# Key transfers shared between two queues, query copies moved to VectorE, and a weight split moved by one pass

## What is computed

```python
qr, qi, kr, ki, v = (heads(x @ W.T) for W in (Wqr, Wqi, Wkr, Wki, Wv))
sr = (einsum('bhqd,bhkd->bhqk', qr, kr) + einsum('bhqd,bhkd->bhqk', qi, ki)) * scale
si = (einsum('bhqd,bhkd->bhqk', qi, kr) - einsum('bhqd,bhkd->bhqk', qr, ki)) * scale
probs = softmax(sqrt(sr * sr + si * si)); ctx = einsum('bhqk,bhkd->bhqd', probs, v)
...
h = h + magnitude_attention(layernorm(h))
h = h + ffn(layernorm(h))      # causal attention, then top-2 routing to 8 experts
```

## Time and profile before

| | |
|---|---|
| time, median of 3 runs | 1024.96 us (1017.67 to 1029.4) |
| profiled execution | 1020.74 us, of which the span is 1018.8 us |
| mean granted TensorE clock | 0.919 of full speed |
| TensorE busy | 897.8 us (88%) |
| VectorE, ScalarE busy | 648.8 us, 651.1 us (64% each) |
| GpSimd busy | 482.7 us (47%) |
| magnitude passes 0 to 7 | about 60 us to 372 us of the span |

### The profile page before, as it was taken

The page is one execution under the profiler, slowest core; times in us unless marked ns, Lnnn a source line. Parts: engine busy times, 40 slices in busy tenths (PEclk is TensorE's granted clock), DMA queues, the critical chain, the costliest instruction groups (busy, mean ns, idle before and its releaser), DMA issues.

```text
span 1018.8 us, 21578 instructions
## 1 busy us (share of the span) xinstructions
PE 897.8 (88%) x7037; PEld 699.2 (69%) x7038; DVE 648.8 (64%) x3050; ACT 651.1 (64%) x1386; POOL 482.7 (47%) x509
## 2 busy tenths in 40 slices
PE   3377979989889879999999999467999999999996
PEld 2254556556556456677777776256999999999896
DVE  1666889889788677678877766673344344343341
ACT  2047879788789788988988888264345345344441
POOL 7677656643001101143334333405677677677654
PEclk7567999899899789999999999757999999999999
DMA  7234233231010200010111102426455456565442
GB/s 205 58 72 82 44 67 65 42 64 31 18 32 14 52 1 2 2 38 2 38 39 38 38 2 69 74 55 107 62 110 99 78 109 88 89 108 91 54 51 32
DMA packets 63299, 59.11 MB, mean 58 GB/s; under 512 B 17471, under 2 KB 54242, under 8 KB 63202
## 3 DMA queue, kind: packets, MB, share of 16 engines
q0 software_dynamic: 25344, 27.89, 19.5%
q1 hardware_dynamic: 37666, 29.76, 11.3%
q10 hardware_dynamic: 192, 0.26, 0.1%
HBM read 35.18 MB, written 16.39 MB: 51 GB/s over the span
## 4 chain that ended last, share of the span: by engine, by line
PE 62%; DVE 13%; SPq 6%; ACT 6%; POOL 5%; issue 4%; DMA 2%; POOLq 0%; DVEq 0%; ACTq 0%
PE ps_scores L776 14%; PE ps_ring L768 11%; PE ps_ring L1044 10%; PE ps_ring L776 6%; SPq L500 5%; PE ps_scores L886 5%; PE ps_ctx L903 5%; PE ps_scores L1044 4%; PE ps_scores L889 4%; POOL got L590 3%; DVE probs L1420 2%; ACT probs L1146 1%; DVE probs L1414 1%; ACT square L1137 1%; DMA k<-k_signed 1%
## 5 line engine op out<-in xcount | busy, mean ns | idle before, releaser
L1260 ACT ACTIVATE probs<-ps_scores,fc_bias 128x512 f32<-128x512 f32 (+1 forms) x144 | 88.9, 617 | 171.5 <-PE ps_scores L776 167.6
L650 POOL DMA_INDIRECT out<-z_t,slots_now x80 | 128.1, 1601 | 83.2 <-DVE z_t L1761 58.9
L768 PE MATMUL ps_ring<-ident,probs 128*128 128x128 f32 x768 | 127.2, 291 | 17.2 <-ACT q L1101 8.0
L1128 ACT ACTIVATE prob_t<-ps_ring 128x512 f32<-128x512 f32 x192 | 114.5, 598 | 37.0 <-PE ps_ring L768 36.3
L1137 ACT ACTIVATE square<-ps_scores 128x512 f32<-128x512 f32 x192 | 104.6, 600 | 29.4 <-PE ps_scores L886 24.2
L1153 ACT ACTIVATE probs<-probs,neg_max 128x128 f32<-128x128 f32 x384 | 120.8, 397 | 2.6 <-DVE neg_max L1420 2.6
L768 PEld LDWEIGHTS ps_ring<-ident,probs 128*128 128x128 f32 x768 | 90.5, 147 | 43.4 <-issue 13.0
L1420 DVE CUSTOM_DVE_ANT_0 probs<-ps_scores,causal 128x128 f32<-128x128 f32 x384 | 88.6, 286 | 40.8 <-PE ps_scores L889 40.5
L1044 PE MATMUL ps_ring<-work,probs 128*128 128x192 f32 x672 | 114.5, 326 | 0.0
L1044 PEld LDWEIGHTS ps_ring<-work,probs 128*128 128x128 f32 x672 | 109.3, 190 | 0.1
L1414 DVE CUSTOM_DVE_ANT_0 probs<-square 128x128 f32<-128x128 f32 x384 | 89.2, 287 | 30.6 <-ACT square L1137 30.1
(11 more groups left out here) (230 smaller groups left out, 2056.1 us busy)
## 6 DMA issues: line engine op xcount, KB each, us to landing
k<-k_signed SPq DMA_DIRECT2D x176, 32.0 KB
work<-pj_w SPq DMA_DIRECT2D x8, 576.0 KB, 4.9
token_in<-xin SPq DMA_DIRECT2D x8, 384.0 KB, 3.4
out<-resid SPq DMA_DIRECT2D x8, 384.0 KB, 4.3
vals<-fc_w SPq DMA_DIRECT2D x8, 384.0 KB, 3.5
vals<-fc_w SPq DMA_DIRECT2D x16, 192.0 KB, 4.1
out<-z_t,slots_now POOLq DMA_INDIRECT x80, 3.6
token_in<-xin SPq DMA_DIRECT2D x8, 128.0 KB, 4.3
```

What stands on the lines that cost most here:

```text
L650: gp.indirect_dma_start(out[:, :], bass.IndirectOffsetOnAxis(slots_now[:, u, 1, t:t + 1], 0), slot_y[:, o, :], None, compute_op=ALU.add).t ...
L768: return pe.transpose(dst, src, ident[0:n, 0:n])
L1128: sc.activation(prob_t[:, s % 2, :, :], src.rearrange("p (h q) -> p h q", h=4), ACT.Exp if p is mag else ACT.Copy).then_inc(ring_free[i], 1)
L1260: sc.activation(hidden[:, c % 2, f_, 0:128 * nt], ps_scores[:, i, 0:128 * nt], ACT.Gelu, bias=fc_bias[:, e, f_:f_ + 1]).then_inc(gelu_done ...
```

## The change

Four things are changed.

Of the 24 key transfers of a group, SyncE keeps all eight of block 0 and the first four of blocks 1 and 2. The other four of blocks 1 and 2 are issued by GpSimd (`turn_rest_of_keys`), at the end of its pass, from group 2 on. Those of group 0 and group 1 stay as they were.

The copy of the last queries (`proj` 5) goes from ScalarE to VectorE, and the shifts of the twelve jobs are laid out anew (`SHIFTS`).

The rounding of the causal weights is cut in three pieces and goes to slots 1, 2 and 3 of pass 7 on ScalarE, the remainders to slots 2, 3 and 4 on VectorE, and TensorE waits piece by piece.

For the first causal group the third and fourth projection go from slots 10 and 13 to 9 and 11.

```diff
+SHIFTS = {13: (0,), 14: (1, 2), 15: (3, 4, 5), 0: (6, 7), 1: (8,), 2: (9,), 3: (10,), 4: (11,)}
 CAU_PROJ = (4, 7, 10, 13)
+FIRST_CAU_PROJ = (4, 7, 9, 11)
...
+        def wait_for_turned_keys(eng, b, g):
+            eng.wait_ge(keys_turned[b], 16 * (8 * g if b == 0 else 4 + 4 * g))
+            if b > 0 and g > 1:
+                eng.wait_ge(late_turned[b - 1], 16 * 4 * (g - 1))
...
@@ SyncE
-                    for quarter, part in product(range(4), range(2)):
+                    for quarter, part in product(range(4 if b == 0 or g == 1 else 2), range(2)):
...
@@ GpSimd, one_pass
                     if fetched is not None and fetched < GROUPS:
                         gather_step(fetched, slot)
+                if 2 <= p + 1 < GROUPS:
+                    turn_rest_of_keys(p + 1)
+
+            def turn_rest_of_keys(g):
+                for b in range(1, BLOCKS):
+                    pool.wait_ge(keys_signed, BLOCKS * g + b + 1)
+                    for quarter, part in product(range(2, 4), range(2)):
+                        to, of = 32 * quarter + HEAD_DIM * part, 32 * quarter + HEAD_DIM * (1 - part)
+                        gp.dma_start(k_of[g % 2][to:to + HEAD_DIM, b, 1, :, :].rearrange("p s k -> p (s k)"),
+                                     k_signed[of:of + HEAD_DIM, b, :]).then_inc(late_turned[b - 1], 16)
...
@@ TensorE
-                        if p is cau and g == 0:
-                            pe.wait_ge(cau_w_split, 2)
                     if p is cau:
                         m, b = divmod(s, 2)
+                        if g == 0:
+                            pe.wait_ge(cau_w_split, m + 1)
...
@@ ScalarE
-                        kind == "proj" and p is mag and s < 3):
+                        kind == "proj" and p is mag and s in (0, 1, 2, 5)):
                     return
...
+            def causal_weights_high(part):
+                raw_qk, raw_v = raw_weights(cau)
+                if part == 0:
+                    act.wait_ge(cau_w_scaled, 4)
+                    for f in (("proj", 5), ("value", 1)):
+                        i, n = PLACE[GROUPS - 1, f]
+                        act.wait_ge(ring_full[i], n + 1)
+                if part < 2:
+                    sc.activation(w_hi[:, :, part, 0:256], raw_qk[:, :, part, :], ACT.Copy).then_inc(cau_w_high, 1)
+                else:
+                    sc.activation(v_hi[:, :, 0:HID], raw_v, ACT.Copy).then_inc(cau_w_high, 1)
...
+                    if p == GROUPS - 1 and 1 <= slot <= 3:
+                        causal_weights_high(slot - 1)
...
-                    split_weights_high(cau_w_scaled, 4, cau_w_high, cau)
...
@@ VectorE
+                elif kind == "proj" and p is mag and s == 5:
+                    dve.wait_ge(ring_full[i], n + 1)
+                    ve.tensor_copy(q_of[number % 2][:, 2, :, :], src.rearrange("p (s k) -> p s k", s=GROUP)
+                                   ).then_inc(free, 1)
...
-                        for j in range(2 * (slot - 13), 2 * (slot - 13) + 2):
+                        for j in SHIFTS[slot]:
                             shift_rows(now, j)
...
+                    if p == GROUPS - 1 and 2 <= slot <= 4:
+                        causal_weights_low(slot - 2)
...
-                    split_weights_low(cau_w_loaded, cau_w_high, cau_w_split, cau)
```

More of the change, by code:

```diff
@@ L104, in causal_fills @@
         fills += [(what, s)] if s is not None else []
-    fills += [("proj", k) for k in range(4) if at == CAU_PROJ[k] - STEPS]
+    fills += [("proj", k) for k in range(4) if at == (FIRST_CAU_PROJ if number == GROUPS else CAU_PROJ)[k] - STEPS]
     fills += [("value", k) for k in range(4) if at == CAU_VALUE[k] - STEPS]
@@ L343, in tower_kernel @@
         keys_turned = [sem(f"keys_turned{b}") for b in range(BLOCKS)]
+        late_turned = [sem(f"late_turned{b}") for b in range(1, BLOCKS)]
         sign_made = sem("sign_made")
@@ L821, in fill @@
                         taken_out(number, ("xT", 0), ("xT", 1))
+                        if p is cau and g == 0:
+                            pe.wait_ge(cau_w_split, 3)
                     for t in range(p.values_per_fill):
@@ L873, in scores @@
                     if g > 0:
-                        pe.wait_ge(keys_turned[j], 8 * 16 * g)
+                        wait_for_turned_keys(pe, j, g)
                     else:
@@ L1200, in one_pass @@
                             turn_rest_of_keys()
+                    if p == GROUPS - 1 and 1 <= slot <= 3:
+                        causal_weights_high(slot - 1)
                     if ready is not None and slot >= 3 and slot % 3 == 0 and slot // 3 <= GROUP:
                         copy_ctx(*phase_of(ready), slot // 3 - 1)
-                if p == GROUPS - 2:
-                    for f in (("proj", 5), ("value", 1)):
-                        i, n = PLACE[GROUPS - 1, f]
-                        act.wait_ge(ring_full[i], n + 1)
-                    split_weights_high(cau_w_scaled, 4, cau_w_high, cau)
             def copy_domains():
@@ L1345, in fill @@
                     elif g > 1:
-                        dve.wait_ge(keys_turned[s], 8 * 16 * (g - 1))
+                        wait_for_turned_keys(dve, s, g - 1)
                     ve.tensor_scalar(k_signed[:, s, :], k[:, s, 0, :, :].rearrange("p s k -> p (s k)"), sign[:, 0:1],
@@ L1605, in split_weights, with causal_weights_low @@
                                  ).then_inc(raw_split, 1)
+            def causal_weights_low(part):
+                raw_qk, raw_v = raw_weights(cau)
+                dve.wait_ge(cau_w_high, part + 1)
+                if part < 2:
+                    ve.tensor_tensor(w_lo[:, :, part, 0:256], raw_qk[:, :, part, :], f(w_hi[:, :, part, 0:256]),
+                                     ALU.subtract).then_inc(cau_w_split, 1)
+                else:
+                    ve.tensor_tensor(v_lo[:, :, 0:HID], raw_v, f(v_hi[:, :, 0:HID]), ALU.subtract
+                                     ).then_inc(cau_w_split, 1)
             def split_first_weights(quarter):
@@ L1629, in one_pass @@
                     if now is not None and now < GROUPS and slot >= 13:
-                        for j in range(2 * (slot - 13), 2 * (slot - 13) + 2):
+                        for j in SHIFTS[slot]:
                             shift_rows(now, j)
-                    if ready is not None and ready < GROUPS and slot < 6:
-                        shift_rows(ready, slot + 6)
+                    if ready is not None and ready < GROUPS and slot < 5:
+                        for j in SHIFTS[slot]:
+                            shift_rows(ready, j)
                     for n, at in ((ready, slot), (before, slot + STEPS)):
```

## The result

The changed kernel takes 1018.59 us in the median (1011.04 to 1025.78, 20 runs); the kernel before took 1024.72 beside it (20 runs). The ratio is 0.9949, 95% interval 0.9928 to 0.9970: 5.2 us faster, where 1025 and no change were forecast. A second comparison, further down, gave 0.9935 (0.9909 to 0.9960).

A forecast was written before the change was run, and what follows sets the result against it. It took TensorE's waits for SyncE's key transfers, ScalarE's query copy and the clock as what could be gained at the borders. Losses of 13.7 us less gains of 12.9 gave +0.8: 1025 us, no measurable change, range 1012 to 1041.

The forecast's parts named there:

- I take somewhat less, 1.10: GpSimd's queue: each plain key transfer costs 1.10 us, so 8.8 us for eight, somewhat under the 1.36 us `word_table` gathers.
- 8.5: Border 1 to 2: GpSimd's late transfers land block 2 at 155.4 where TensorE got it at 146.81, a loss of 8.5 us.
- +0.5, +2.5 and +0.7: Passes 2, 3 and 4: GpSimd's later work, chiefly gathers, moves back behind the transfers, losing 0.5, 2.5 and 0.7 us.
- cheap transfers: Rival: GpSimd transfers at 0.63 us each, clock stays up; 7.1 us gained, 1018 us, or 1012 to 1015; chance 0.2.
- the clock: TensorE's granted clock: stays up at border 4 to 5 (-2.0 us) and 6 to 7 (-2.5), falls at 1 to 2 (+1.5).
- Key waits -3.6: Borders 3 to 4, 4 to 5, 5 to 6: TensorE's three waits for SyncE's key transfers go, 3.6 us gained.
- Query copy -2.0: Borders 0 to 1, 3 to 4, 4 to 5, 5 to 6: ScalarE's copy leaves the row, 0.5 us gained at each.
- I count nothing: Border 2 to 3: group 4's norm, two slots late, waits behind the shifts, so no gain is booked for the query copy.
- Border 6 to 7, -4.7: Weights and query copy off ScalarE's row: -3.2 us, clock -2.5, pieces in slots 1 to 4 +1.0; together 4.7 gained.
- 7 to 8, -0.6: Border 7 to 8: ScalarE's 0.70 us copy of the last causal projection moves to slot 11, where it has room; 0.6 us gained.
- Moments 2.8 us later: Border 1 to 2: group 3's moments begin at 140.5 instead of 137.70, behind VectorE's query copy and three shifts.
- A landing of 2.5: GpSimd's key transfers: the data land 2.5 us after the transfers, a figure used for the block arrivals at border 1 to 2.

The follow-up runs named there:

- second comparison: The changed kernel as it is, timed again against the kernel before on the same chip, beside the later follow-up kernels: ratio 0.9935 (0.9909 to 0.9960).
- half transfers: Changed kernel with each GpSimd key transfer cut in two of half the columns, 16 instead of 8 a group: ratio to the kernel before 1.0032 (1.0008 to 1.0055).
- K alone: Kernel before with only GpSimd's share of the key transfers for blocks 1 and 2, from group 2 on: ratio to it 0.9987 (0.9967 to 1.0007).
- Q: The last query copy on VectorE with the new shifts; as the only change to the kernel before, ratio to it 0.9992 (0.9969 to 1.0015).
- C: Causal weights in three pieces, projections in slots 4, 7, 9, 11; as the only change to the kernel before, ratio to it 0.9970 (0.9949 to 0.9991).
- The kernel without Q: Changed kernel with the last query copy on ScalarE again and the shifts in their old slots: ratio to the kernel before 0.9934 (0.9909 to 0.9959).
- K in the whole: Told by the changed kernel with all 24 key transfers on SyncE again: ratio to the kernel before 1.0017 (0.9992 to 1.0042), 7.0 us slower than the whole change.

## Why the prediction was wrong

**The step that failed** is "I take somewhat less, 1.10" for a transfer of GpSimd. It is 0.49 to 0.51. The bounds were 0.63 below and 1.91 above; the value taken was that of the nearest row of the same engine, a gather over 128 rows, and the true one lay below even the lower bound. Put into the prediction's own sums: block 1 lands at 144.1 + 2.0 + 2.0 = 148.1 instead of 151.0, 4.9 us after it is wanted. That is now the later of the two, since block 2 lands at 150.2 and is wanted, 4.9 us later than before, at 150.6. With the old wait of 1.13 gone, border 1 to 2 costs 3.8 instead of 8.5. The place gathers of pass 3 end in time: in the trace they end at 200.69, the root follows at once and is there at 202.1, and VectorE uses it at 202.56 without a wait:

```profile
199.15 1.54 POOL L599 DMA_INDIRECT got<-place_rows,id_now  x1 [0.30 <-issue]
200.76 0.24 POOL L593 TENSOR_SCALAR rstd<-moments 128x4 f32<-128x4 f32 x1
201.08 1.05 POOL L595 TENSOR_TENSOR rstd<-rstd,half 128x4 f32<-128x4 f32 x1
```

```profile
202.56 1.40 DVE L1563 SCALAR_TENSOR_TENSOR resid<-got,moments,row_c 128x192 f32<-128x192 f32 x4
```

VectorE's waits for roots are 3.7 us in all (5.0 before), so the +0.5, +2.5 and +0.7 are nothing. Together 8.4 us less loss: +0.8 becomes -7.6. The half transfers test this the other way round: at 1.0 us for the same bytes the ratio is 1.0032, no gain at all, as the prediction would have it. The rival "cheap transfers" named this case, with 1018.

**The second step, of the other sign, is the clock.** The prediction saw two places with the clock at 0.50, where the trace has more, and counted -2.0 at border 4 to 5, -2.5 at 6 to 7 and +1.5 at 1 to 2, 3.0 us of net gain. Each single reading came true in the trace (1.00 at the first two, 0.51 at the third). Yet it fell elsewhere: the mean granted clock of 12 executions of the changed kernel was 0.9218, that of 35 of the kernel before on the same chip 0.9215, a difference of 0.0003 with some 0.0024 to each side. At 7 us for 0.01 (last section) 3.0 us of gain would have shown as some 0.004. With nothing for the clock, -7.6 becomes -4.6; measured were -5.2, and -6.6 in the second comparison. That the sum comes so near is in part luck: several of its terms were off, in both directions, as follows.

**By its other terms:**

- *Key waits -3.6.* Right as a size: 3.5 us of idle time went at borders 3 to 6 with K alone. In length the stretch from group 3 to 7 gives 5.2. That K is worth 1.3 us in time alone and 7.0 in the company of Q and C was not foreseen; there the prediction's habit of pricing each part in the timeline of before is at fault. It counted no key wait at border 6 to 7, and one of 1.6 to 2.7 us stands there once the weights are gone.
- *Query copy -2.0.* Its idle time went: 2.0 us at borders 3 to 6 (idle sums 2.3, 2.4, 2.4 with K alone, 1.7 each with all). The kernel without Q is as fast all the same: what Q gains there, it loses with K at border 1 to 2, 2.9 us by the stretches. That the prediction booked this loss under GpSimd's transfers, and not against Q, hid that Q brings the whole nothing. "I count nothing" at border 2 to 3 left out 2.3 us of waiting for group 4's input, net of the waits it replaced 0.7.
- *Border 6 to 7, -4.7, and 7 to 8, -0.6.* From group 7's keys to the end 4.9 us are gained in the trace, 0.4 short of the sum. Over all traces it is 4.0. In time C is worth 3.1 alone and 1.9 in the whole.
- *Moments 2.8 us later.* Right: counted from the mark they begin 12.2 us behind it instead of 9.4, and query copy and three shifts take 2.4 us of that (141.99 to 144.40). That GpSimd's transfers stand behind them was right in kind, and worth 1 to 3 us.
- *A landing of 2.5* was 2.0.

**On the two pages.** The 3100 ns of the Trainium skill ("SBUF — State Buffer", SBUF: two separate sides) were not met: of the 48 transfers the longest took 0.642 us with VectorE busy beside them, and the longest in any run 1.21. Whether VectorE held the shared port pair in one of these moments, no row shows. The 620 ns that the Trainium skill gives for a transfer alone is the nearer price, still above the 492 ns measured. The rule of the Trainium skill that issuing from several engines saves little ("DMA: Bandwidth & Descriptors", Issuing engines are not separate DMA queues) fits the time of K alone (1.3 us) and not K in the whole (7.0 us), nor the 5.2 us from group 3 to 7.

**What stays open:** why K alone gains 1.3 us in time (interval -0.7 to 3.4) where its stretch from group 3 to 7 is 5.2 us shorter; how far C and the keys of group 7 help each other; and how many microseconds of the change are won or lost by where the clock falls, since it moved from run to run.

## What to carry to other kernels

Before you price an operation that the trace does not show by the nearest row of its engine, ask what that row's time consists of: a gather that reads an index per row says little on a plain transfer, and the range between the bounds decided the sign here. Look at what stands ahead of a new piece of work in its engine's order and try it one place earlier: eight transfers moved ahead of a wait, and norm steps moved ahead of shifts, were worth as much again as the change. When a stall is taken away at one place, don't book a gain in clock with it unless the mean clock over many executions moves.

## What the runs showed that was not expected

- A plain transfer costs GpSimd's queue 0.49 us for 32 KB and 0.48 us for 16 KB, less than SyncE's 0.59 (the longest of any run took 1.21); a gather of the same engine costs 1.06 or 1.6.
- The time of one program follows its mean granted clock: over 25 executions of the kernel before on one chip by about 7 us for 0.01 of clock, and the clock went from execution to execution. That is how a profiled pair can show no difference between kernels that are 5 us apart.
- Two microseconds of TensorE standing still, at 200.4, were followed by 10.2 us at half the clock, in a pass that took 5.8 us more. The 5.51 us of standing still that ended at 152.18 had no more around it, 10.2 us at 0.51, and these began within the wait.
- The stretch from group 2 to 3 took 38.0 us in one trace and 42.5 in two others, though these three kernels do not differ up to there.
